# Running all eight experts for 32 of 49 tiles while edges are summed, and combining stored outputs after the choice

## What is computed

```python
# third block: messages by relation, summed over the edges that end in a node
transformed = einsum('ni,rio->rno', layernorm(x), weight)      # 16 relations
x = x + segment_sum(transformed[rel_type, src] * norm, dst)    # 100000 edges

# fourth block, xn = layernorm(x), N = 6250 nodes, D = 256, F = 512, E = 8 experts
logits = mean(xn, over all nodes) @ Wr + br                    # one row of 8
weights = softmax(softmax(logits) * scale)                     # scale from a capacity
top_w, top_i = top_k(weights, 2); top_w = softmax(top_w)       # the same two for all nodes
h = gelu(xn @ W1[e] + b1[e]);  y_e = h @ W2[e] + b2[e]
out = layernorm(sum_e top_w[e] * y_e + xn) * gamma + beta
x = x + out
```

## Time and profile before

| | us |
|---|---|
| median of 3 runs | 4308.29 (4297.85 to 4309.88) |
| the profiled execution | 4302.73, of which its span 4301.0 |
| search and attention | 2452.9 |
| relations | 1374.4 |
| choose_two | 55.2 |
| feed_forward | 418.5 |

### The profile page before, as it was taken

The page is one execution under the profiler, slowest core; times in us unless marked ns, Lnnn a source line. Parts: engine busy times, 40 slices in busy tenths (PEclk is TensorE's granted clock), DMA queues, the critical chain, the costliest instruction groups (busy, mean ns, idle before and its releaser), DMA issues. The chain is left out here.

```text
span 4301.0 us, 37015 instructions
## 1 busy us (share of the span) xinstructions
PE 2179.5 (51%) x7603; PEld 1366.5 (32%) x7603; DVE 1745.9 (41%) x3846; ACT 730.5 (17%) x1456; POOL 1757.3 (41%) x1827
## 2 busy tenths in 40 slices
PE   3437978788877767666679700000000000037996
PEld 2324545444544444443346300000000000034665
DVE  4664434444434444444341134333343243332545
ACT  1212222222222222221122300000000000002332
POOL 4374333343433433344430165555555655510111
PEclk7768988888988888887789955555555555558998
DMA  5633333333333333333331432222222322200000
GB/s 165 184 84 92 102 100 112 101 106 109 114 99 95 112 103 106 100 103 97 100 101 69 153 95 80 80 81 79 80 75 71 87 76 78 81 18 25 20 15 26
DMA packets 196109, 384.26 MB, mean 89 GB/s; under 512 B 46330, under 2 KB 88786, under 8 KB 195858
## 3 DMA queue, kind: packets, MB, share of 16 engines
q0 software_dynamic: 84736, 232.41, 19.7%
q1 hardware_dynamic: 111122, 149.64, 10.0%
HBM read 252.14 MB, written 129.75 MB: 89 GB/s over the span
## 5 line engine op out<-in xcount | busy, mean ns | idle before, releaser
L806 POOL DMA_INDIRECT gat_rows<-h_table,idx x799 | 777.4, 973 | 1110.3 <-DVE gat_acc L1212 859.1
L1363 POOL DMA_INDIRECT rel_rows<-transformed,rel_idx x799 | 755.2, 945 | 565.9 <-issue 565.9
L1027 PE MATMUL bank<-tr_wr,tr_xt 128*128 128x512 f32 x1568 | 786.4, 641 | 260.1 <-ACT tr_xt L873 178.6
L1535 PE MATMUL bank<-weight,rec 128*128 128x1 f32 x196 | 42.0, 352 | 1381.5 <-DVE weight L1561 1381.5
L1027 PEld LDWEIGHTS bank<-tr_wr,tr_xt 128*128 128x128 f32 x1568 | 311.7, 204 | 591.0 <-issue 372.9
L994 PE MATMUL bank<-mo_xt,mo_w 128*128 128x256 f32 (+1 forms) x1600 | 457.7, 408 | 57.6 <-issue 56.4
L1535 PEld LDWEIGHTS bank<-weight,rec 128*128 128x128 f32 x196 | 41.9, 333 | 1382.3 <-DVE weight L1561 1382.3
L1438 DVE SCALAR_TENSOR_TENSOR bank<-rel_rows,rel_now,bank 128x256 f32<-128x256 f32 x823 | 403.1, 490 | 181.8 <-issue 103.0
L1012 PE MATMUL bank<-mo_w,mo_ht 128*128 128x256 f32 x1568 | 397.8, 396 | 88.7 <-issue 69.5
L902 ACT ACTIVATE tr_row<-bank 128x512 f32<-128x512 f32 x392 | 232.8, 597 | 1100.5 <-PE bank L1027 543.9
L1188 DVE TENSOR_TENSOR gat_rows<-gat_rows 128x1024 f32<-128x1024 f32 (+1 forms) x169 | 254.6, 1530 | 302.8 <-ACT gat_rows L852 302.8
(11 more groups left out here) (280 smaller groups left out, 1966.5 us busy)
## 6 DMA issues: line engine op xcount, KB each, us to landing
transformed<-tr_row SPq DMA_DIRECT2D x392, 256.0 KB
gat_rows<-h_table,idx POOLq DMA_INDIRECT x799
rel_rows<-transformed,rel_idx POOLq DMA_INDIRECT x799
h_table<-hrow SPq DMA_DIRECT2D x49, 132.0 KB, 1.9
records<-xa SPq DMA_DIRECT2D x49, 132.0 KB
rec<-x_moved SPq DMA_DIRECT2D x1, 6272.0 KB
x_moved<-tr_x SPq DMA_DIRECT2D x24, 256.0 KB, 2.2
tr_wr<-L_gnn_weight SPq DMA_DIRECT2D x2, 2048.0 KB, 22.0
```

Source lines behind the costliest of these rows:

```text
L806: pool.indirect_dma_start(out=rows[:, column(u, j), :], out_offset=None, in_=p.h_table[:], in_offset=bass.IndirectOffsetOnAxis(ap=idx[u][: ...
L1027: ins = pe.matmul(p.bank[6 + c % 2][:], xt2[:, k, u * P:(u + 1) * P], wr[:, k, m * CW:(m + 1) * CW], start=(k == 0), stop=(k == KD - 1))
L1363: pool.indirect_dma_start(out=rows[b][:, j, :], out_offset=None, in_=p.transformed[:], in_offset=bass.IndirectOffsetOnAxis(ap=idx[b][:, j: ...
```

## The change

- `relations` keeps two gather buffers with a shared middle instead of three separate ones (48 columns instead of 96), as `attention` does. POOL starts a tile when the tile two before it is summed, and the tile's 17th and later columns when the tile before it is summed (`summed`). The loop is two tiles long. The lists of indices are now copied by DVE (`idx[u]`), when it sees the gathers landed.
- DVE also adds `beta` to the first 32 tiles' rows, which SP stores (`x3b`), and once in two tiles works out the reciprocal root of the variances by three Newton steps (`spread_of`, 15 small operations and a copy).
- At the same time PE runs all eight experts over tiles 0 to 31 in eight groups of four tiles: 8 transposes, 64 matmuls of 512 columns and 128 of 256 columns in a group. ACT norms the tiles, copies the transposes (summing them for the mean on the way), does 32 gelus of 512 columns and 32 copies of 256 columns in a group and issues 32 stores of 128 KB to `ys` and one of 512 KB to `xn_table`. SP loads all eight experts at the start (8 MB).
- `choose_two` sums only the last 17 tiles with PE (34 matmuls); the roots are there already.
- `feed_forward` runs PE for 17 tiles (five groups). For the other 32, SP loads the two chosen experts' stored outputs, the normed rows and `x + beta` (four transfers of 512 KB for four tiles), and DVE combines them. 13 batches in the order D D D T D D T D D T D T T (D: four stored tiles, T: tiles through PE). POOL adds the biases ahead of DVE, then scatters the batch before. The Newton root replaces ACT's.

The core of the diff:

```diff
 def relations(p: Program):
-    BUFFERS = 3
+    PAIRS, SHARED = NT // 2, WIN // 2
+    WIDTH = 2 * WIN - SHARED
-        rows = [sb(f"rel_rows{b}", [P, WIN, D], F32) for b in range(BUFFERS)]
+        rows = sb("rel_rows", [P, WIDTH, D], F32)
         @block.gpsimd
-                pool.wait_ge(idx_ready[b], i + 1)
-                pool.wait_ge(used[b], i + 1)
+                pool.wait_ge(idx_ready[u], i + 1)
                 def gather(s):
+                    if s == 0:
+                        pool.wait_ge(summed, t + 1)
+                    if AT1[s] == SHARED:
+                        pool.wait_ge(summed, t + 2)
                     for j in range(AT1[s], AT1[s] + COLS1[s]):
+        @block.tensor
+            def into(g, e, f):
+                at_least(pe, gelued, g * LOCAL + n - 1)
+                for k in range(KD):
+                    ins = pe.matmul(p.bank[3 + n % 2][:], w1[:, e, k, f * P:(f + 1) * P], xt[:, k, :], ...)
+            def outof(g, e, j):
+                for f in range(F):
+                    ins = pe.matmul(p.bank[5 + m % 3][:, 0:D], ht[:, e % 2 * F + f, j * P:(j + 1) * P], w2[:, e * F + f, :], ...)
+            def group(g, last=False):
+                for e in range(E1):
+                    for f in range(F):
+                        into(g, e, f)
+                        if e >= 1:
+                            outof(g, e - 1, f)
         @block.vector
                 dve.wait_ge(gathered[u], until)
+                dve.tensor_copy(idx[u][:], p.win[:, bass.ds(t + 2, 1), 0:WIN]...).then_inc(idx_ready[u], 1)
 ...
-                chain_m(dve.tensor_tensor(tile_row(p, t), total, tile_row(p, t), ALU.add), True)
-                dve.sem_inc(used[b], 1)
+                chain_m(dve.tensor_tensor(x, total, x, ALU.add), True)
+                dve.sem_inc(summed, 1)
+                if not tail:
+                    dve.wait_ge(x3_out[u], 16 * (i + 1))
+                    dve.tensor_tensor(x3b[u][:], x, beta[:], ALU.add).then_inc(x3b_ready, 1)
+            def spread_of(i, t, n):
+                inverse_root(chain_p, dve, mo[:, :, 1], root[:, 0, :], root[:, 1, :], root_i[:], root[:, 2, :])
+                chain_p(dve.tensor_tensor(mo[:, 0:n, 2], root[:, 2, 0:n], valid[:, bass.ds(t, n)], ALU.mult))
+                chain_p(dve.scalar_tensor_tensor(mo[:, :, 3], mo[:, :, 0], -1.0, mo[:, :, 2], ALU.mult, ALU.mult), True)
+                dve.tensor_copy(p.ms[:, bass.ds(t, n), :], mo[:, 0:n, :]).then_inc(x3_done, 1)
 def choose_two(p: Program):
-            for t in range(NT):
+            for t in range(TAIL):
 def feed_forward(p: Program):
+                if kind == "done":
+                    for j in range(n):
+                        ins = dve.scalar_tensor_tensor(y[s][:, j, :], ye[s][1][:, j, :], p.two_w[:, 1:2], y[s][:, j, :], ALU.mult, ALU.add)
+def inverse_root(chain, dve, var, v, h, i, r):
+    chain(dve.tensor_scalar(v, var, EPS, None, ALU.add))
+    chain(dve.tensor_scalar(h, v, -0.5, None, ALU.mult))
+    chain(dve.tensor_scalar(i, v.bitcast(I32), 1, None, ALU.arith_shift_right))
+    chain(dve.tensor_scalar(r.bitcast(I32), i, -1.0, float(0x5F3759DF), ALU.mult, ALU.add))
+    for n in range(3):
+        chain(dve.tensor_tensor(v, r, r, ALU.mult))
+        chain(dve.tensor_tensor(v, v, h, ALU.mult))
+        chain(dve.scalar_tensor_tensor(r, v, 1.5, r, ALU.add, ALU.mult))
```

More of the change, by code:

```diff
@@ L121, in __init__ @@
         self.ms = self.keep("ms", [P, NT, 4], F32)
+        self.sums = self.keep("sums", [P, GROUPS * KD], F32)
         self.passed = self.sem("passed")
@@ new lines, in group @@
+            def group(g, last=False):
+                for e in range(E1):
+                    for f in range(F):
+                        gelu(g, e, f)
+                        if e >= 1:
+                            evacuate(g, e - 1, f)
+                    if e >= E1 - G and not last:
+                        norm(g + 1, e - (E1 - G))
+                if not last:
+                    copies(g + 1)
+                for j in range(G):
+                    evacuate(g, E1 - 1, j)
+            for j in range(G):
+                norm(0, j)
@@ L1410, in _ @@
+            copies(0)
+            group(0)
+            with act.Fori(1, GROUPS - 1) as g:
+                group(g)
+            group(GROUPS - 1, True)
+            act.wait_ge(xn_out, 16 * GROUPS)
+            for j in range(G):
+                act.wait_ge(stored[j], 16 * GROUPS * E1)
         @block.vector
@@ new lines, in _, with pair @@
+            dve.wait_ge(x_in[0], 16)
+            for u in range(2):
+                dve.sem_inc(x3_out[u], 16)
+            def pair(i):
+                for u in range(2):
+                    t = 2 * i + u
+                    tile(i, u, t, t, False)
+                spread_of(i, 2 * i, 2)
+            with dve.Fori(0, DONE // 2) as i:
+                pair(i)
+            with dve.Fori(DONE // 2, PAIRS) as i:
+                for u in range(2):
+                    t = 2 * i + u
+                    tile(i, u, t, t - DONE, True)
+                spread_of(i, 2 * i, 2)
@@ new lines, in feed_forward, with size, units, loads @@
+        loaded = [p.sem(f"ff_loaded{s}") for s in range(2)]
+        stored = [p.sem(f"ff_stored{s}") for s in range(2)]
+        block = ctx.enter_context(nc.Block())
+        def size(kind, n):
+            return G if kind == "done" else TAILS[n][1] - TAILS[n][0]
+        def units(b):
+            return sum(size(*BATCHES[i]) for i in range(b))
+        def loads(b):
+            return sum(1 for i in range(b) if BATCHES[i][0] == "done" and i % 2 == b % 2)
+        def tails(b):
+            return sum(1 for i in range(b) if BATCHES[i][0] == "tail")
@@ L1761, in _ @@
+            norm(0)
+            norm(1)
+            act.wait_ge(b1_turned, 1)
+            act.activation(b1[:], p.bank[7][:, 0:EF], ACT.Copy).then_inc(b1_ready, 1)
+            act.wait_ge(b1_ready, 1)
+            for g in range(len(TAILS)):
+                copies(g)
+                gelus(g)
+                if g + 2 < len(TAILS):
+                    norm(g + 2)
         @block.vector
         def _(dve):
-            first = Chain(p, dve, setup)
-            for s in (normed, taken, varied, finished):
-                dve.sem_inc(s, U)
```

613 lines of the change are left out of this document (359 added, 254 removed).

## The result

On the chip of the first runs the changed kernel took 4442.77 us in the median (4406.93 to 4470.2, four runs) against 4306.17 (4297.85 to 4309.88, four runs): a ratio of 1.032, 95% interval 1.028 to 1.037. It is **slower by 3.2%**, where 4185 was forecast and 4310 was the upper end. The profiled execution took 4423.15, its span is 4421.4.

A forecast was written before the change was run, and what follows sets the result against it. `relations` was taken as bound by POOL's gathers plus fast DVE work left when POOL stops. 4302.7 + 124 (`relations`) - 30 (`choose_two`) - 213 (`feed_forward`) = 4184, stated as 4185 us, range 4060 to 4310.

The forecast's parts named there:

- growth past +190: Rival: `relations` grows by over 190 us without a stall in every tile, 4250 to 4350 in all; chance 0.08.
- the full stall in every tile: Rival: POOL waits for DVE in every tile of `relations`, 859 us in place of 326, total 4570; chance 0.08.
- The cycle of POOL and DVE: In `relations`, DVE's added work is left for POOL's stops, once in two tiles: +147 us, at worst +189.
- The small-growth rival: Rival: in `relations` stalls come once a tile and DVE's work fits between, -20 to +30 us, 4040 to 4090; chance 0.13.
- I cost all this at nothing: In `relations`, PE's and ACT's expert work, stores, loads and tables hide under POOL's and DVE's cycle: 0 us.
- ACT is not the bound: In `relations`, ACT needs some 2.3 us per quarter of an expert against PE's 3.5, so it doesn't bound.
- PE the bound: Rival: PE at half clock takes 225 us a group, `relations` 1920, total 4605; chance 0.04.
- choose_two: This stage sums 68 records instead of 196 and drops the root: -30 us, to near 25.
- feed_forward: This stage falls to 205 us, -213, with DVE bounding it; bounds 190 and 235.
- PE ends early: In `feed_forward`, PE has 17 tiles left, 120 us of work, and so finishes ahead of DVE.
- The crawl ends: Rival: DVE's slow stretches in `relations` come from the three buffers or branch layout and vanish, total 3785; chance 0.05.
- Slower: The whole kernel comes out slower than before, beyond the 4295 to 4321 that counts as the same; chance 0.13.

The follow-up runs named there:

- e18: The changed kernel without expert work on PE and ACT in `relations`, on a stalling chip: 4290.2 us against 4337.7 for the kernel before.
- e10: The changed kernel itself, unaltered, run again on a smooth chip: 3220.5 us against 3364.7 for the kernel before, ratio 0.957.
- e15: The kernel before itself, unaltered, run again on a smooth chip: 3366.0 us against 3366.8.

## Why the prediction was wrong, step by step

The miss on the first chip, by stages from barrier to barrier (the prediction's share of each in brackets): ahead of `relations` -13.6 (0), `relations` +315.4 (+124), `choose_two` -29.4 (-30), `feed_forward` -152.0 (-213), together +120.4 (-119). No rival's range holds the 4443 that were measured: growth past +190 ended at 4350, the full stall in every tile stood at 4570.

- **The cycle of POOL and DVE**: right in mechanism, near in size. Gathers stayed 1.25 us apart. POOL's stops over 2 us grew from 314 to 493 us on the first chip, by 179 where 147 was forecast and 189 the bound; from 275 to 524 on the second, which is past the bound. They came 37 times in 49 tiles on the first chip and 29 times on the second, where once in two is 24. Up to the last edge sum `relations` took 1532.4, +158 against +124. e18 shows it without PE: -47.5 in all; with -29.5 and -151.4 for the last two stages, +133 is left for `relations` and what lies ahead. The small-growth rival doesn't hold on the smooth chips either: +40.3, where it ended at +30. What was not seen is what makes DVE slow while POOL gathers: its register instructions (above), of which the change adds 448 to 1994.
- **"I cost all this at nothing"** is the step that failed. The price of a group was taken from `feed_forward`, where nothing gathers: 115 us. That price is right where the chip doesn't stall (115 on the smooth chip, e10) and for the last group, after the gathers (4007 to 4128.5, 121 us), and wrong by nearly two under the gathers of this one. Matmuls of 512 columns took 664 ns against 595 on the smooth chip, at a granted clock of 0.77 against 0.92, but the larger part is waiting for PE's signals to ACT, up to some 37 us late. The margin named, 175 us a group, was passed by over 30 (209 in the mean of seven): eight groups ended 157.5 us behind the edge sums. The margin was drawn a little too wide besides: 120 + 8 x 175 is 1520, past the 1498 forecast for the stage. The row that could have warned is in the trace of before, in `attention`, the one stage where PE, ACT and POOL work together. ACT's longest entry there, and the same stage on a smooth chip below it:

```profile
ACT tr_row L902 <- remote: 496.1, 40, 31.6
```
```profile
ACT tr_row L902 <- PE bank L1027: 554.2, 275, 5.8
```

  I used `attention` for POOL's waits and not for PE's and ACT's pace beside them.
- **"ACT is not the bound"** by 2.3 us against 3.5: right as work, wrong as a chain. PE and ACT exchange two signals a quarter expert, some 64 a group from PE to ACT, and it was the exchange that was slow.
- **PE the bound** (4605, chance 0.04) came true in kind: matmuls reach the end of `relations`. Its reason, half clock, did not: the granted clock was 0.77 under the gathers and 1.00 behind them.
- **choose_two**: 25.5 us, forecast near 25.
- **feed_forward**: the sum of DVE's work and starts was right, 205 forecast and 199.8 once the ring is cut. "PE ends early" was the failed part: it went by PE's busy time and not by what releases ACT's norms. 267.4 is outside the bound of 235.
- **The crawl ends** (3785, chance 0.05) was taken for a matter of buffers and branches. It goes with the chip: on a smooth one the kernel before has `relations` at 1035.1 and the changed one 1075.4, near that rival's 999 + 100. Its total of 3785 doesn't fit there, since what lies ahead of `relations` is shorter on such a chip too (1855 us instead of 2452).
- **Slower**, 0.13 in all, was too little: the forecast of "faster" rested on a cover whose price came from a stage without gathers. On the smooth chips the stages came to +40 - 29 - 152, and faster it was.

## What to carry to other kernels

Price work that is moved under another stage from a stretch in which both kinds of work already run together; if the trace has one, look there at the moved engines' waits, not only at their busy time. A handshake between two engines has a price of its own: count how many signals the moved work exchanges, and ask what each costs beside what it is moved under. And when a buffer is reused, follow who must be done with it through every engine's queue, since a double buffer whose release lies behind three other engines is a ring, not a cover.

## What was not expected of the hardware

- Chips of one type differ by 28% on one program: 3365 and 4306 us for the kernel before, each steady to some tenths of a per cent, and only in stages with indirect gathers. In `relations` gathers, gelus and adds take the same time on both (946, 687, 490 ns). In `attention` a gather takes even less on the stalling chip, 973 ns against 1129 (e15).
- On the stalling chips DVE's register and branch instructions took 0.70 or 1.40 us in stretches where POOL gathered (364 of 1994 in `relations` before, none over 0.21 on the smooth chip). Over the stage that is 312 us of DVE's time, with its waits and loads.
- On a stalling chip PE's signals to ACT came up to some 37 us late while POOL gathered, and those that had piled up all within 0.4 us, in the one case shown 5.8 us after POOL stopped. Of the 89 increments by PE recorded from 3971 on, with the gathers over, none was late. ACT's signals to PE were prompt (0.05 us in the case shown).
- A change can be 4.3% faster on one chip and 3.2 to 4.6% slower on another. Runs beside each other on one chip give the ratio for that chip; whether it holds for another kind, they don't say.
